# Graph attention on one core: group 0 loaded in halves, probabilities moved off GpSimd, group 1's v in other PSUM banks

## The reference

```python
h = maximum(layernorm(x), 0)
v, q, k = h @ weight, h @ wq, h @ wk
alpha = maximum(q @ k.T, 0) * (adj != 0)
alpha = softmax(alpha, axis=1)          # over the query index n of [b, n, m]
out = x + alpha @ v
```

## Time and profile before

| | |
|---|---|
| median of 3 runs | 421.05 us (421.01 to 421.43) |
| profiled execution | 420.8 us, of which span 419.0 us |
| PE busy | 406.6 us (97%) |
| DVE busy | 282.9 us (68%) |
| ACT busy | 253.3 us (60%) |
| POOL busy | 298.2 us (71%) |
| DMA | 73.97 MB, mean 177 GB/s |

### The profile page before, as it was taken

One profiled execution on the slowest core, in us unless ns is written; L12 is line 12 of the kernel. 1 busy time (PEld: TensorE's weight loads), 2 busy tenths in 40 slices (PEclk: granted clock), 3 DMA queues, 4 the chain that ended last, 5 costly groups with the idle time before them and its releaser, 6 DMA issues.

```text
span 419.0 us, 9187 instructions
## 1 busy us (share of the span) xinstructions
PE 406.6 (97%) x3499; PEld 314.8 (75%) x3499; DVE 282.9 (68%) x504; ACT 253.3 (60%) x517; POOL 298.2 (71%) x315
## 2 busy tenths in 40 slices
PE   5999997999999999999999999999999999999996
PEld 4434543779889797979889797979889797978452
DVE  4786566475866768685876768676777677456353
ACT  4478774657485666667485666667586765523421
POOL 0379887979979797979879797979889796130320
PEclk9999999999999999999999999999999999999999
DMA  7965748996969797896978598996988599261022
GB/s 286 364 91 97 194 81 212 202 219 177 191 216 178 221 165 206 199 210 178 196 238 157 154 213 219 194 207 180 187 251 151 157 228 221 51 107 59 0 103 100
DMA packets 157368, 73.97 MB, mean 177 GB/s; under 512 B 131216, under 2 KB 139408, under 8 KB 157328
## 3 DMA queue, kind: packets, MB, share of 16 engines
q1 hardware_dynamic: 156752, 72.37, 75.5%
q10 hardware_dynamic: 576, 1.05, 0.7%
HBM read 24.12 MB, written 16.78 MB: 98 GB/s over the span
## 4 chain that ended last, share of the span: by engine, by line
PE 81%; POOL 9%; DMA 3%; DVE 3%; ACT 1%; SPq 1%; issue 1%; DVEq 0%; POOLq 0%; ACTq 0%
PE bank L1041 9%; PE bank L1027 9%; PE bank L1026 9%; PE bank L1042 9%; PE bank L1024 9%; PE bank L1039 9%; PE s_bank L1055 3%; PE s_bank L1053 3%; PE s_bank L1054 3%; POOL hn_lo L375 2%; PE bank L1060 2%; PE bank L1062 2%; PE bank L1061 2%; DMA x_sb<-in_x 2%; POOL hn_lo L401 2%; PE bank L1160 2%
## 5 line engine op out<-in xcount | busy, mean ns | idle before, releaser
L375 POOL TENSOR_TENSOR hn_lo<-h,hn_hi 128x512 f16<-128x512 f32 x64 | 73.4, 1159 | 41.0 <-ACT hn_hi L512 40.7
L502 ACT ACTIVATE h<-x_sb,shift,rstd 128x512 f32<-128x512 f32 x64 | 49.8, 803 | 51.4 <-POOL shift L370 51.4
L401 POOL TENSOR_TENSOR hn_lo<-s,hn_hi 128x512 f16<-128x512 f32 x52 | 58.6, 1159 | 0.0
L1024 PE MATMUL bank<-hT_hi,mt_hi 128*128 128x256 f16 x208 | 56.7, 273 | 0.0
L1027 PE MATMUL bank<-hT_hi,mt_lo 128*128 128x256 f16 x208 | 56.7, 273 | 0.0
L1041 PE MATMUL bank<-wt_lo,hT_hi 128*128 128x256 f16 x208 | 56.7, 273 | 0.0
L1042 PE MATMUL bank<-wt_hi,hT_lo 128*128 128x256 f16 x208 | 56.7, 273 | 0.0
L1026 PE MATMUL bank<-hT_lo,mt_hi 128*128 128x256 f16 x208 | 56.7, 273 | 0.0
L1039 PE MATMUL bank<-wt_hi,hT_hi 128*128 128x256 f16 x208 | 56.7, 273 | 0.0
L517 ACT ACTIVATE hn_hi<-s 128x512 f16<-128x512 f32 x52 | 32.5, 628 | 36.4 <-POOL s L390 23.9
L407 POOL TENSOR_TENSOR probs<-exps,row_inv 128x512 f32<-128x512 f32 x16 | 16.8, 1049 | 47.3 <-DVE row_inv L829 47.3
(11 more groups left out here) (142 smaller groups left out, 1153.4 us busy)
## 6 DMA issues: line engine op xcount, KB each, us to landing
x_sb<-in_x SPq DMA_DIRECT2D x16, 1024.0 KB, 5.5
out_h<-x_sb SPq DMA_DIRECT2D x64, 256.0 KB, 2.1
adj_sb<-in_adj SPq DMA_DIRECT2D x16, 256.0 KB, 5.4
w_sb<-in_L_gnn_weight SPq DMA_DIRECT2D x1, 1024.0 KB, 11.4
hn_lo<-in_L_gnn_wk ACTq DMA_DIRECT2D x2, 256.0 KB, 3.9
hn_lo<-in_L_gnn_wk SPq DMA_DIRECT2D x2, 256.0 KB, 3.7
hn_hi<-in_L_gnn_wq SPq DMA_DIRECT2D x2, 256.0 KB, 6.3
hn_hi<-in_L_gnn_wq ACTq DMA_DIRECT2D x2, 256.0 KB, 6.9
```

The costliest lines, as they stand in the source:

```text
L375: nc.gpsimd.tensor_tensor(hn_lo[:, s, b], h[:, b], hn_hi[:, s, b], ALU.subtract).then_inc(h_split, 1)
L401: nc.gpsimd.tensor_tensor(low, s32[:, f], high, ALU.subtract).then_inc(s_split, 1)
L502: nc.scalar.activation(h[:, b], x_sb[:, s, b], ACT.Relu, bias=shift[:, b:b + 1], scale=rstd[:, b:b + 1]).then_inc(h_made, 1)
L1024: nc.tensor.matmul(o, bh[:, k, cols], ah[:, :, k], start=first and c == 0 and k == 0, stop=False, skip_group_check=True)
```

## The change

It has five parts.

1. PE does 12 transposes of the identity into `top_bank` before the first weights are there; nobody reads them. The order of the head's products changes: each product of M is done in halves, and the transposes of the next quarter of Wq stand between them.
2. x of group 0 and W are loaded in two DMAs each, with a semaphore for each half. Statistics and maxima follow the halves; the layernorm scales of group 0 are made for two graphs at a time (`first_scales`). Group 0's transposes: graphs 0 and 1 one by one, graphs 2 and 3 in one DMA for hi and one for lo; the hi DMA waits only for the hi part.
3. `normalise` goes from GpSimd. ACT makes `p_hi` (`hi_of_p`: four activations with `row_inv` as scale), DVE `p_lo` (`lo_of_p`: four operations exps x row_inv - p_hi). `probs` is gone. In a period ACT does it between `copy_p5_v` and `hi_of_t11`, DVE between the aggregates and `lo_of_t`.
4. Group 1's v goes into banks 0 to 3, where its t was; each product waits for the lo part of t from its bank, and the scores of group 1 for all residuals of group 0. Period 2 starts once three of four `v_lo` are there.
5. Orders in ACT's and DVE's programs between the groups 0 and 3 change to suit.

```diff
+        def v_bank(g):
+
+            return M_BANK if g == 1 else [bank[VB][:], bank[VE][:], bank[FREE][:], bank[TA][:]]
...
+            def transpose_first(b, n, landed):
+
+                sp.wait_ge(h_hi_made, b + n)
+                sp.dma_start_transpose(hT_hi[:, 0, b:b + n].rearrange("p b k n -> p (b k) n"),
+                                       hn_hi[:, 0, b:b + n].rearrange("p b d -> p (b d)")).then_inc(landed, 16)
+                sp.wait_ge(h_split, b + n)
...
-            load_x(0)
-            sp.dma_start(w_sb[:], weight.rearrange("(k p) d -> p k d", p=N)).then_inc(w_loaded, 16)
+            for b in (0, HG):
+                sp.dma_start(x_sb[:, 0, b:b + HG], x_dram[:, b:b + HG, :]).then_inc(x0_loaded[b // HG], 16)
+            for k in (0, HK):
+                sp.dma_start(w_sb[:, k:k + HK], weight.rearrange("(k p) d -> p k d", p=N)[:, k:k + HK]).then_inc(w_loaded[k // HK], 16)
             load_adj(0)
             load_x(1)
             load_adj(1)
             load_x(2)
-            for b in range(GB):
-                transpose_first(b)
+            transpose_first(0, 1, hT0_landed[0])
+            transpose_first(1, 1, hT0_landed[1])
+            transpose_first(2, 2, hT0_landed[2])
...
+            def first_scales(f):
+
+                c = slice(HG * f, HG * (f + 1))
+                pool.wait_ge(meanvar_made, HG * (f + 1))
+                nc.gpsimd.tensor_tensor(var_eps[:, c], mean_var[:, c, 1], eps[:, c], ALU.add).then_inc(ln_step, 1)
+                nc.gpsimd.tensor_tensor(neg_mean[:, c], mean_var[:, c, 0], minus_one[:, c], ALU.mult).then_inc(ln_step, 1)
+                pool.wait_ge(ln_step, 4 * f + 2)
+                nc.gpsimd.tensor_tensor(inv_std[:, c], var_eps[:, c], minus_half[:, c], ALU.pow).then_inc(ln_step, 1)
+                pool.wait_ge(ln_step, 4 * f + 3)
+                nc.gpsimd.tensor_tensor(rstd[:, c], inv_std[:, c], h_scale[:, c], ALU.mult).then_inc(ln_step, 1)
+                pool.wait_ge(ln_step, 4 * f + 4)
+                nc.gpsimd.tensor_tensor(shift[:, c], neg_mean[:, c], rstd[:, c], ALU.mult).then_inc(rstd_made, 1)
...
-            def normalise(g):
-
-                inv = row_inv[:].unsqueeze(2).to_broadcast([N, GB, N])
-                pool.wait_ge(inv_made, g + 1)
-                nc.gpsimd.tensor_tensor(probs[:], exps[:], inv, ALU.mult).then_inc(probs_made, 1)
-                if later(g):
-                    pool.wait_ge(out_filled, GB * g)
-                nc.gpsimd.tensor_tensor(p_hi[:], exps[:], inv, ALU.mult).then_inc(probs_made, 1)
-                pool.wait_ge(probs_made, 2 * g + 2)
-                nc.gpsimd.tensor_tensor(p_lo[:], probs[:], p_hi[:], ALU.subtract).then_inc(p_split, 1)
...
             def period(g, j):
-                normalise(g - 1)
                 layernorm_scales(g + 2)
                 sums_of_h(g + 2, j % 2)
                 lows_of_sums(g + 2, j % 2)
...
+            def hi_of_p(g):
+
+                act.wait_ge(inv_made, g + 1)
+                if later(g):
+                    act.wait_ge(out_filled, GB * g)
+                for b in range(GB):
+                    nc.scalar.activation(p_hi[:, b], exps[:, b], ACT.Copy, scale=row_inv[:, b:b + 1]).then_inc(p_hi_made, 1)
+
             def period(i, j, nxt2=True, nxt2_sums=True):
 
                 g = i * UNROLL + j
@@ -622,6 +638,7 @@
                 copy_p5_t(g)
                 copy_p1_v(g)
                 copy_p5_v(g)
+                hi_of_p(g - 1)
                 hi_of_t11(g)
...
             exponentials(0)
             act.wait_ge(hT0_landed[2], 2 * 16)
             hi_of_h(2, 0, 2)
-            act.wait_ge(hT0_landed[3], 2 * 16)
             hi_of_h(2, 0, 3)
+            hi_of_p(0)
             hi_of_whole_t(1, 0)
             act.wait_ge(mt_summed, 4)
             for f in range(4):
@@ -717,17 +734,20 @@
             hi_of_sum(2, 0, 0, S1)
             hi_of_sum(2, 0, 1, S3)
             hi_of_whole_t(1, 2)
+            hi_of_whole_t(1, 3)
             hi_of_sum(2, 0, 2, S2)
             hi_of_sum(2, 0, 3, S4)
-            hi_of_whole_t(1, 3)
             hi_of_whole_v(1, 0)
-            for b in range(GB):
-                normalise_h(3, 3, b)
-                if b > 0:
-                    hi_of_h(3, 1, b - 1, turn(0, 1))
-            hi_of_h(3, 1, GB - 1)
+            normalise_h(3, 3, 0)
+            normalise_h(3, 3, 1)
             hi_of_whole_v(1, 1)
+            hi_of_h(3, 1, 0, turn(0, 1))
+            hi_of_h(3, 1, 1)
+            normalise_h(3, 3, 2)
             hi_of_whole_v(1, 2)
+            hi_of_h(3, 1, 2)
+            normalise_h(3, 3, 3)
+            hi_of_h(3, 1, 3)
             hi_of_sum(3, 1, 0, S1)
             hi_of_sum(3, 1, 1, S3)
             hi_of_whole_v(1, 3)
...
+            def lo_of_p(g):
+
+                for b in range(GB):
+                    vec.wait_ge(p_hi_made, GB * g + b + 1)
+                    nc.vector.scalar_tensor_tensor(p_lo[:, b], exps[:, b], row_inv[:, b:b + 1], p_hi[:, b], ALU.mult,
+                                                   ALU.subtract).then_inc(p_split, 1)
...
+                lo_of_p(g - 1)
                 lo_of_t(g, 0, bank[TA][:], 0, 0)
...
-                stats_all(0, 0, b)
-            vec.wait_ge(w_loaded, 16)
-            weight_max(w_sb[:], w_max[:, 0])
-
-            vec.wait_ge(w_maxed, 2 * K + 1)
+                stats_first(b)
+            for k in range(2):
+                vec.wait_ge(w_loaded[k], 16)
+                weight_max(w_sb[:, HK * k:HK * (k + 1)], w_max[:, 0, HK * k:HK * (k + 1)])
+
+            vec.wait_ge(w_maxed, 2 * K + 2)
...
+            lo_of_wt(2)
             softmax_sum(0)
+            lo_of_p(0)
             lo_of_whole_t(1, 0)
+            lo_of_wt(3)
...
+            lo_of_mt(0)
+            lo_of_mt(1)
+            lo_of_whole_v(1, 0)
+            lo_of_mt(2)
+            lo_of_mt(3)
             make_mask(2, 0, 2)
-            for b in range(GB):
+            for b in range(1, GB):
                 lo_of_whole_v(1, b)
...
+
+            for k in range(WARM):
+                nc.tensor.transpose(top_bank[:, N * (k % K):N * (k % K + 1)], ident[:], ident[:])
             for r in range(K):
                 transpose_wk(r)
+
             transpose_wq(0)
+            product_m(0, range(2))
             transpose_wq(1)
-            product_m(0)
+            product_m(0, range(2, K))
             transpose_wq(2)
+            product_m(1, range(2))
             transpose_wq(3)
-            product_m(1)
+            product_m(1, range(2, K))
...
-            pe.wait_ge(t_split, K + 1)
-            for b in range(GB):
-                pe.wait_ge(out_read, b + 1)
+            for b in range(GB):
+                pe.wait_ge(t_split, K + b + 1)
                 whole_product_v(1, b)
+
+            pe.wait_ge(out_read, GB)
             scores(1, 1, quadrants=False)
 
-            pe.wait_ge(v_split, 2 * GB)
+            pe.wait_ge(v_split, GB + TE + 1)
```

More of the change, by code:

```diff
@@ L178, in graph_attention_kernel @@
         top_bank = bank[FREE]
+        x0_loaded = [sem(f"x0_loaded{k}") for k in range(2)]
         x_loaded = [sem(f"x_loaded{s}") for s in range(UNROLL)]
@@ L182, in graph_attention_kernel @@
         stored = [sem(f"stored{s}") for s in range(UNROLL)]
-        w_loaded = sem("w_loaded")
+        w_loaded = [sem(f"w_loaded{k}") for k in range(2)]
         wq_loaded = [sem(f"wq_loaded{r}") for r in range(K)]
@@ L232, in graph_attention_kernel @@
         s_split = sem("s_split")
-        hT0_landed = [sem(f"hT0_landed{b}") for b in range(GB)]
+        hT0_landed = [sem(f"hT0_landed{b}") for b in range(3)]
         hT_landed = [sem(f"hT_landed{s}") for s in range(2)]
@@ L434, in _ @@
             pool.wait_ge(consts_made, 5)
[L435 removed]
+            first_scales(0)
+            first_scales(1)
             for b in range(GB):
@@ L477, in _ @@
                     period(g, g)
-                else:
-                    normalise(g - 1)
-                    if g + 2 == LAST:
-                        layernorm_scales(LAST)
-                        for b in range(GB):
-                            lo_of_h(LAST, LAST % 2, b)
-            normalise(LAST - 1)
-            normalise(LAST)
+                elif g + 2 == LAST:
+                    layernorm_scales(LAST)
+                    for b in range(GB):
+                        lo_of_h(LAST, LAST % 2, b)
         @block.scalar
@@ L494, in normalise_h @@
             def normalise_h(g, s, b):
-                act.wait_ge(rstd_made, g + 1)
+                act.wait_ge(rstd_made, 1 if isinstance(g, int) and g == 0 and b < HG else g + 2)
                 if isinstance(g, int) and g <= FIRST:
@@ L601, in hi_of_whole_v @@
                     act.wait_ge(out_filled, GB * g)
-                nc.scalar.activation(v_hi[:, b], V_BANK[b], ACT.Copy, scale=T_SCALE).then_inc(v_hi_made, 1)
+                nc.scalar.activation(v_hi[:, b], v_bank(g)[b], ACT.Copy, scale=T_SCALE).then_inc(v_hi_made, 1)
             def hi_of_whole_t(g, c):
```

(38 more changed lines are left out.)

52 lines of the change are left out of this document (25 added, 27 removed).

## The result

The changed kernel takes **417.34 us** (median of 4 runs, 417.14 to 417.66), the kernel before 421.1 beside it: ratio 0.991, 95% interval 0.9893 to 0.9927. A second set of 5 runs gave 417.68 against 421.51, ratio 0.9913 (0.9899 to 0.9926). The forecast was 417.1 with a range of 416.0 to 419.2. The profiled execution took 417.14, its span 415.3 (before 420.8 and 419.0).

A forecast was written before the change was run, and what follows sets the result against it. TensorE, busy 97% of the span, bounds the kernel, so gains lie in the first 90 us. Gaps 4.75 + head 0.17 - new stalls 1.0 = 3.9 less than the 421.05 median: 417.1 us, range 416.0 to 419.2.

The forecast's parts named there:

- the four old gaps: Four TensorE waits before 90 us, by starts 1.02, 2.83, 0.57 and 0.33, claimed to go: 4.75 us.
- Part 1: Head: idle transposes bring the faster pace forward, product 0 starts at 9.2, f32 stream ends 24.94 for 25.11: net -0.17.
- The 0.44 for wq1: Head: wq1's four transposes leave the shadow of ACT's copy and stand alone between half products: +0.44 us.
- rival A: Head: the faster pace comes no earlier, f32 ends at 25.55, 0.6 gained for 1.2: 417.7 us; chance 0.12.
- Part 2: Group 0's loads and transposes: h at 16.5, graphs 2 and 3 landed by 28.7, the 1.02 wait gone.
- Part 3: Group 1's v in t's banks: waits of 2.83 and 0.57 go, TensorE enters period 2 at 74.3, not 78.93.
- Part 4 in the prologue: Probabilities on ACT (1.4 us) and DVE (1.0 us) before the loop: 1.0 us of new stalls in period 2.
- Rival B: Group 3's ACT and GpSimd chain is longer, with p_hi at 0.48 and more serial steps: 418.8 us; chance 0.11.
- Part 4 in the loop: Thirteen periods: ACT and DVE take the probabilities in idle time, lo_of_t starts at 183.15: 0 us a period.
- the bank's 0.34: Loop: the first residual frees its bank 0.34 us before the fourth out wants it.
- Rival C: Loop: the first residual frees the bank too late, 0.5 us in each of 13 periods: 423.6 us; chance 0.07.
- Part 5: End of the kernel: p_hi of the last two groups fits between waiting work; last stores stay: 0 us.

The follow-up runs named there:

- second profile: The changed kernel run once more, unedited, on the chip of three later runs: 417.68 us, span 415.9.
- first profile: The changed kernel's first profiled execution, unedited: 417.14 us, span 415.3.
- experiment 2: The changed kernel with the head's products in the old order, idle transposes kept: 416.93 us, ratio 0.9897 to the kernel before.
- experiment 1: The changed kernel without the twelve idle transposes: 418.07 us, ratio 0.9929 to the kernel before.
- experiment 3: The changed kernel with x of group 0 and W loaded whole, in one load each: 418.54 us, ratio 0.9934 to the kernel before.
- experiment 8: The changed kernel with GpSimd held back, in group 0 alone, until p_lo is done: 419.67 us, ratio 0.9951 to the kernel before.
- experiment 11: The changed kernel with p_lo computed twice in each looped period, the second into an unread tile: 418.78 us, ratio 0.9936 to the kernel before.

## Why the prediction was right, point by point

The number, 417.1 for 417.34, is closer than its terms. Against the second profile the head came as forecast and the four old gaps went, but the new stalls are 1.84 instead of 1.0; the first profile's lucky head and the spread from execution to execution cover the rest.

**Part 1** was right in its figures, with luck in the first profile, and its cause stays open. The f32 stream ends at 24.91 in the second (24.94 predicted). The 0.44 for wq1 was real (experiment 2 gets it back). The faster pace was there before Wq's transposes, and product 0 starts at 9.16; rival A, no earlier pace, would have read 9.8. But experiment 1 has that pace before Wq's transposes too, with no idle ones ahead. So that the twelve idle transposes brought it forward is not shown.

**Part 2** was right in its sum and open in its parts. `h` starts at 16.00 (16.5 predicted), and experiments 2 and 3 show that ACT's copies of Wq set this: it moves with the order of the products (14.43) and not with the loads (16.54). The pair's last transpose lands at 29.27 (28.7), 0.4 before TensorE comes for it at 29.69. From issue to landing it took 4.6 where the prediction took 3.4, near the upper bound of 4.8, but it was issued 0.6 earlier (24.66 for 25.3). The wait of 1.02 is gone; the change has 0.4 us of room there.

**Part 3** was right: v(1) starts at 60.86, the 2.83 went but for 0.25 at the second `tT_lo`, which the prediction had at 61.3 and the trace has at 63.6: `p_lo(0)`, below, stands ahead of it on DVE, and in experiment 8, where that is short, the gap is not there. Undone, the part costs 5.7 us, not 3: a wait of 4.6 and 1.8 of slow clock, less some of the later waits. The prediction took a wait to cost its length, and for the 2.83 of the kernel before that held, since the clock stayed.

**Part 4 in the prologue** held in its sum (new stalls of 1.0 within period 2, with the entry free) for a reason that was half wrong. `p_hi` was 0.29 behind one another, four in 1.26 us for the 1.4 predicted; the estimate of 0.29 each from the Trainium skill's figures (ScalarE: Activation LUTs, What ACT_TABLE_LOAD costs) agrees. The term that failed is "I take 0.25, 1.0 in all" for `p_lo(0)`: 4.33 us were measured, and its upper end, 0.54 each, was too low as well. The rule of shared ports stood in the prediction, but it was weighed only for the loop, where GpSimd waits or makes its four-column scales at that time; in the prologue GpSimd works on 512 columns from 52.9 to 63. The cost was small only because TensorE wanted `p_lo` at 58.27 and had it at 58.02. DVE's line behind it is late, and so the entry to period 2 takes 0.3 (1.39 in the first profile), which the prediction had free; the copies of t and v and the fourth `out` take 0.64, 0.26 and 0.37 where 0.2, 0.25 and 0.55 were foreseen. In all 1.6 in period 2 instead of 1.0, and with the 0.25 of part 3, 1.84. The head's extra 0.4 of the first profile hid about half of this miss. Rival B's sign is in the second profile: ACT's copy of t is done at 80.71, past 80.5, and TensorE waits 0.64 for it. B was right that this chain is longer than counted, but not by how much (it had 2.7 of stalls), nor by its cause (`p_hi` at 0.48): `p_hi` took 0.29, and GpSimd's two `lo_of_h` beside DVE's `mt_lo` took 3.48.

**Part 4 in the loop** gave 0 a period, as forecast, but the prediction was wrong on the slack. The steady period of the changed kernel, ACT, DVE and PE, against the earlier trace rows:
```profile
172.55 0.49 ACT L602 ACTIVATE exps<-alpha,shift_max,s_unscale 128x128 f32<-128x128 f32 x1 [0.39 <-DVE shift_max L841]
...
176.00 1.27 ACT L626 ACTIVATE p_hi<-exps,row_inv 128x128 f16<-128x128 f32 x4
...
176.39 0.43 DVE L828 TENSOR_SCALAR mask<-adj_sb 128x512 bf16<-128x512 int32 x1
...
177.02 1.11 DVE L858 SCALAR_TENSOR_TENSOR p_lo<-exps,row_inv,p_hi 128x128 f16<-128x128 f32 x4
178.04 0.68 DVE L795 SCALAR_TENSOR_TENSOR tT_lo<-bank,tT_hi 128x512 f16<-128x512 f32 x1
...
180.75 0.70 DVE L817 TENSOR_TENSOR bank<-bank,spare 128x512 f32<-128x512 f32 x1 [1.41 <-PE bank L1092]
181.40 0.75 DVE L863 SCALAR_TENSOR_TENSOR x_sb<-bank,out_unscale,x_sb 128x512 f32<-128x512 f32 x1
...
182.49 0.38 PE L1110 MATMUL bank<-v_hi,p_hi 128*128 128x512 f16 x1
```
The residual stands 1.09 before the fourth `out`, as before (186.14 - 185.05), so the bank's 0.34 is unchanged. But the sum for v now idles 1.41 us where 0.36 stood, in spite of `p_lo`. The mask takes 0.43 instead of 1.03 to 1.19, as foreseen; and the first exponential starts 9.9 us before the fourth `out`, not 8.4 (186.14 - 177.74; it is the one ahead of the row at 178.23). The step that failed is "the scales come 1.4 earlier; nobody waits for them". By the rows they end 2.6 earlier against TensorE, and `h` and GpSimd's sums with them; ACT's last copy of v stands behind the copy of a sum and comes 1.5 earlier (13.0 before the fourth `out` for 11.5), and so do `v_lo`, the shift and the exponentials behind it. ACT's wait for the scales fell from 51.4 to 20.9 us in the whole span. This round of the loop is read from the rows; no experiment moved the scales alone. Rival C had no ground: experiment 11 puts twice the load there for nothing. (DVE and ACT had 6.5 and 8.0 us free in the window of the earlier trace rows, not 6.8 and 8.3; nothing hangs on it.)

**Part 5**, the end: 4.4 us from the last matmul's start to the span's end before and after.
